# A new global order of all steps in a two-block transformer kernel, with 66 instead of 428 filler matmuls

## What is computed

```python
x = L0_attn_x                                   # (16, 256, 128)
x = _layernorm(x + attn(x))                     # block 1
x = _layernorm(x + ffn(x))                      # block 2, seen as tokens in groups of (s, h) = (128, 128)

def attn(x):                                    # 16 query heads, 4 key/value heads, 8 wide
    q, k = rope(rms_norm(x @ w_q)), rope(rms_norm(x @ w_k)); v = x @ w_v
    s = tanh(q @ k.T / sqrt(8) / 50) * 50       # causal
    return (softmax(s) @ v) @ w_o

def ffn(x):                                     # 16 heads, not causal, then 8 experts
    hn = layernorm(x) * ln1_g + ln1_b
    x = x + softmax(q @ k.T / sqrt(8)) @ v @ wo + bo     # q, k, v from hn
    hn2 = layernorm(x) * ln2_g + ln2_b
    idx = argmax(hn2 @ gate_w + gate_b)         # one expert of 8 for each token
    return x + (relu(hn2 @ w1[idx] + b1[idx]) @ w2[idx] + b2[idx])
```

## Time and profile before

| | before |
|---|---|
| median of 3 runs | 726.37 us (725.46 to 730.91) |
| span of the profiled execution | 701.0 us |
| busy: PE / DVE / ACT / POOL | 570.1 / 480.9 / 425.4 / 416.7 us |
| TensorE matmuls | 5771 |
| mean granted TensorE clock | 0.927 |

### The profile page before, as it was taken

How to read it: one execution, slowest core, us unless ns; L and a number is a source line. 1 busy time by engine, 2 the same in 40 slices (tenths; PEclk the granted TensorE clock), 3 DMA queues, 4 the chain that set the end, 5 groups by cost and what they waited for, 6 DMA issues and landing times.

```text
span 701.0 us, 16358 instructions
## 1 busy us (share of the span) xinstructions
PE 570.1 (81%) x5771; PEld 339.1 (48%) x5771; DVE 480.9 (69%) x1356; ACT 425.4 (61%) x650; POOL 416.7 (59%) x443
## 2 busy tenths in 40 slices
PE   2648888888888878888897898878997899888992
PEld 1324333344445444455454554545553555557992
DVE  3546757868678868587867768687777787635452
ACT  1675376676785666757677596756675654534661
POOL 2469573648486953775757585769544235525664
PEclk9969779899999988799999999899998999999996
DMA  6420000000000100000012301001002022186650
GB/s 146 135 69 2 8 1 9 2 24 1 9 2 25 40 2 6 5 16 10 17 41 62 85 9 36 1 20 60 25 29 62 12 69 91 39 257 183 187 149 6
DMA packets 30143, 34.30 MB, mean 49 GB/s; under 512 B 6970, under 2 KB 21984, under 8 KB 30064
## 3 DMA queue, kind: packets, MB, share of 16 engines
q1 hardware_dynamic: 26096, 25.53, 12.9%
q0 software_dynamic: 2816, 6.43, 2.6%
q10 hardware_dynamic: 1152, 1.30, 0.6%
HBM read 22.37 MB, written 11.27 MB: 48 GB/s over the span
## 4 chain that ended last, share of the span: by engine, by line
PE 40%; DVE 23%; POOL 16%; issue 10%; ACT 7%; SPq 2%; DMA 1%; POOLq 0%; ACTq 0%; DVEq 0%
DVE mx L1230 10%; PE out L877 6%; POOL rs L1411 5%; PE ring_s L863 3%; POOL stack L1414 3%; PE out L762 3%; PE ring_p L943 3%; PE ring_p L701 3%; PE ring_s L843 3%; POOL p L1430 2%; ACT p L1004 2%; PE ring_p L814 2%; ACT p L973 2%; PE ring_s L749 2%; PE ring_p L931 1%
## 5 line engine op out<-in xcount | busy, mean ns | idle before, releaser
L1230 DVE TENSOR_REDUCE mx<-ring_s 128x4 f32<-128x1024 f32 x128 | 152.8, 1218 | 26.9 <-PE ring_s L843 26.1
L1004 ACT ACTIVATE p<-ring_s 128x1024 f32<-128x1024 f32 x128 | 126.3, 1027 | 38.8 <-PE ring_s L863 38.3
L973 ACT ACTIVATE p<-ring_s 128x1024 f32<-128x1024 f32 x96 | 97.1, 1022 | 38.5 <-PE ring_s L749 38.1
L1411 POOL TENSOR_TENSOR rs<-ms,small 128x40 f32<-128x40 f32 x14 | 94.8, 6772 | 27.6 <-DVE ms L1093 27.3
L1414 POOL TENSOR_SCALAR stack<-stack 128x256 f16<-128x256 f16 (+1 forms) x96 | 65.0, 700 | 75.7 <-DVE stack L1222 42.8
L1430 POOL TENSOR_SCALAR_AFFINE_SELECT p<-p 128x512 f32<-128x512 f32 (+1 forms) x96 | 75.8, 798 | 56.4 <-ACT p L977 56.3
L977 ACT ACTIVATE p<-p 128x1024 f32<-128x1024 f32 x96 | 100.2, 1057 | 0.7
L701 PE MATMUL ring_p<-blank 128*128 128x256 f16 x362 | 80.6, 286 | 5.1 <-ACT t_midT L1037 1.9
L877 PE MATMUL out<-p,v 128*32 128x256 f32 x1024 | 69.8, 400 | 1.3 <-DVE rb L1288 1.2
L843 PE MATMUL ring_s<-kc,qs 32*128 32x256 f16 x512 | 51.2, 281 | 20.2 <-DVE mx L1230 13.0
L863 PE MATMUL ring_s<-qs,kc 32*128 32x256 f16 x512 | 49.4, 290 | 10.1 <-DMA qs<-mT 4.5
(11 more groups left out here) (162 smaller groups left out, 1111.5 us busy)
## 6 DMA issues: line engine op xcount, KB each, us to landing
w_up<-in_L_ffn_w SPq DMA_DIRECT2D x40, 256.0 KB, 2.8
t_row<-routed_rows SPq DMA_DIRECT2D x40, 132.0 KB, 2.4
routed_rows<-padrow SPq DMA_DIRECT2D x8, 396.0 KB, 3.2
xs<-in_L_attn_x SPq DMA_DIRECT2D x16, 128.0 KB, 2.2
routed_rows<-padrow SPq DMA_DIRECT2D x8, 132.0 KB, 1.9
qs<-mT SPq DMA_DIRECT2D x64, 2.0 KB
out<-t_y,t_idx POOLq DMA_INDIRECT x40, 2.4
b_down<-in_L_ffn_b SPq DMA_DIRECT2D x1, 512.0 KB, 4.8
```

What stands on the lines that cost most here:

```text
L973: nc.scalar.activation(p1[:, u], bank(f"b_sc{u}", n)[:], ACT.Tanh, scale=float(ISQ / CAP)).then_inc(b_s.sem, 1)
L1004: nc.scalar.activation(p2[:, u], bank(f"e_sc{u}", n)[:], ACT.Exp, scale=float(ISQ)).then_inc(e_s.sem, 1)
L1230: nc.vector.tensor_reduce(mx2[:, t, 2 * pair:2 * pair + 2, 2 * k:2 * k + 2], bank(f"d_mx{j}", n)[:].rearrange("p (z g s) -> p z g s", z=2, ...
L1411: nc.gpsimd.tensor_tensor(rs1[:], ms1[:], half, ALU.pow).then_inc(a_p.sem, 1)
```

## The change

`ORDER` is replaced by another one for the same steps. The list has 2481 entries in place of 2843: 66 `w_fill` in place of 428, and each other step once as before. With the fillers left out of both lists, a TensorE step stands 2.0 places from where it stood on the mean (21 at most), a DVE step 1.3, an ACT step 1.5, a POOL step 2.0 and an SP step 2.4. Neither the plans, the rings, the buffers nor any computation is changed.

In `g_row` the wait for scatters is now made for each slot and not only for a plan's first: for the two latest `f_scatter` that stand ahead of it in the order. `scattered` collects them.

The diff, cut to the lists that the prediction speaks of (the others are replaced in the same way):

```diff
--- before.py
+++ after.py
@@ -121,190 +121,171 @@
 ORDER = {
-    "w_fill": (10, 29, 30, 42, 49, 60, 67, 88, 99, 100, 112, 136, 152, 154, 159, 164, 169, 181, 185, 197, 202, 203,
-        206, 209, 214, 240, 241, 282, 284, 296, 297, 298, 301, 302, 303, 305, 309, 310, 314, 323, 325, 326, 331, 342,
...
-    "a_pow": (82, 168, 275, 396, 516, 658, 884, 978, 1167, 1283, 1519, 1639, 1822, 1957),
-    "f_place": (409, 532, 684, 835, 977, 1134, 1289, 1433, 1621, 1853, 2008, 2127, 2286, 2376, 2508, 2591),
-    "f_scatter": (477, 732, 878, 879, 1122, 1317, 1413, 1444, 1854, 2005, 2033, 2126, 2400, 2427, 2519, 2598),
-    "p_plan": (1442, 2134, 2512, 2605),
-    "g_w": (1472, 1482, 1567, 1574, 1590, 1611, 1699, 1744, 1765, 2139, 2159, 2175, 2332, 2340, 2341, 2352, 2387,
-        2505, 2515, 2570, 2578, 2589, 2600, 2607, 2608, 2648, 2651, 2676, 2681, 2690, 2697, 2715, 2722, 2737, 2757,
-        2780, 2784, 2801, 2814, 2821),
-    "g_row": (1473, 1481, 1486, 1560, 1572, 1599, 1643, 1726, 1759, 2106, 2166, 2171, 2200, 2331, 2342, 2359, 2366,
-        2526, 2528, 2545, 2572, 2583, 2595, 2612, 2618, 2634, 2641, 2642, 2660, 2680, 2692, 2699, 2701, 2714, 2738,
-        2742, 2768, 2772, 2789, 2822),
-    "g_up": (1521, 1523, 1661, 1828, 1902, 1951, 1973, 2076, 2132, 2260, 2315, 2336, 2383, 2426, 2451, 2465, 2504,
-        2563, 2564, 2603, 2614, 2617, 2637, 2644, 2667, 2677, 2683, 2687, 2706, 2718, 2726, 2743, 2755, 2764, 2774,
-        2792, 2795, 2806, 2817, 2824),
-    "g_down": (1608, 1632, 1771, 1842, 1972, 2068, 2079, 2105, 2168, 2289, 2373, 2415, 2421, 2463, 2510, 2533, 2548,
-        2590, 2604, 2615, 2624, 2639, 2646, 2668, 2678, 2685, 2696, 2719, 2724, 2728, 2750, 2756, 2769, 2783, 2793,
-        2802, 2812, 2819, 2828, 2837),
-    "q_sp": (2552,),
...
+    "w_fill": (14, 69, 88, 89, 90, 107, 112, 165, 216, 236, 246, 270, 271, 291, 329, 370, 423, 527, 528, 546, 561,
+        574, 580, 628, 645, 675, 718, 753, 862, 895, 913, 915, 1059, 1060, 1122, 1241, 1269, 1308, 1348, 1366, 1458,
+        1510, 1511, 1543, 1544, 1547, 1642, 1684, 1685, 1686, 1824, 1831, 1851, 1861, 1899, 1913, 1914, 2113, 2149,
+        2228, 2257, 2266, 2267, 2269, 2349, 2468),
+    "a_pow": (72, 148, 231, 392, 492, 615, 760, 867, 1007, 1146, 1272, 1410, 1569, 1653),
+    "f_place": (378, 490, 625, 755, 872, 1001, 1120, 1235, 1409, 1575, 1734, 1835, 1987, 2080, 2161, 2241),
+    "f_scatter": (516, 570, 671, 810, 974, 1006, 1144, 1252, 1495, 1762, 1828, 1839, 2005, 2097, 2168, 2252),
+    "p_plan": (1236, 1841, 2163, 2245),
+    "g_w": (1265, 1283, 1264, 1538, 1263, 1539, 1364, 1413, 1341, 1957, 2009, 1846, 1848, 2032, 1879, 1881, 2033,
+        2177, 2178, 2187, 2184, 2219, 2188, 2250, 2251, 2255, 2295, 2294, 2318, 2292, 2319, 2329, 2354, 2331, 2360,
+        2368, 2367, 2390, 2429, 2455),
+    "g_row": (1267, 1281, 1282, 1340, 1362, 1363, 1365, 1399, 1412, 1847, 1849, 1850, 1880, 1935, 1939, 1950, 1956,
+        2169, 2179, 2185, 2186, 2212, 2220, 2253, 2256, 2293, 2298, 2299, 2316, 2324, 2330, 2332, 2353, 2355, 2357,
+        2366, 2384, 2387, 2408, 2453),
+    "g_up": (1310, 1311, 1441, 1576, 1637, 1667, 1707, 1786, 1855, 1981, 2013, 2030, 2068, 2091, 2123, 2156, 2174,
+        2218, 2222, 2244, 2268, 2270, 2282, 2286, 2307, 2314, 2321, 2339, 2351, 2359, 2373, 2383, 2396, 2405, 2413,
+        2421, 2427, 2437, 2451, 2469),
+    "g_down": (1394, 1401, 1532, 1592, 1690, 1771, 1793, 1809, 1878, 2008, 2059, 2078, 2093, 2135, 2164, 2189, 2197,
+        2236, 2258, 2259, 2273, 2287, 2291, 2308, 2322, 2333, 2342, 2356, 2371, 2378, 2394, 2403, 2412, 2418, 2434,
+        2443, 2450, 2452, 2470, 2476),
+    "q_sp": (2217,),
...
@@ -588,6 +569,13 @@
             elif name in ON_TENSOR or name[:4] in ("b_sc", "d_mx", "e_sc"):
                 shape = "full"
 
+        scattered, so_far = {}, []
+        for name, n in order:
+            if name == "f_scatter":
+                so_far.append(n)
+            elif name == "g_row":
+                scattered[n] = tuple(so_far)
+
         def bank(name, n):
             k = ring_of(name, n)
             return ring[k][turn[name, n] % RINGS[k]]
@@ -642,10 +630,9 @@
             def g_row(s):
                 k = plan_of(s)
                 sp.wait_ge(r_v.sem, r_v.upto(k, "row"))
+                for n in scattered[s][-2:]:
+                    wait_turn(sp, rows_out[n % 2], n, 2, 16 * T)
                 if s == PLANS[k][1]:
-                    last = PLANS[k][0]
-                    for n in (last - 1, last):
-                        wait_turn(sp, rows_out[n % 2], n, 2, 16 * T)
                     if k >= LAST:
                         sp.wait_ge(pads_out, 16 * E)
                         sp.wait_ge(idle_rows, 16 * IDLE)
```

More of the change, by code:

```diff
@@ new lines @@
+    "g_rs": (1437, 1500, 1620, 1643, 1761, 1779, 1819, 1840, 2037, 2046, 2096, 2132, 2137, 2165, 2182, 2201, 2224,
+        2242, 2262, 2276, 2283, 2297, 2301, 2323, 2338, 2343, 2350, 2370, 2381, 2388, 2400, 2410, 2420, 2432, 2441,
+        2448, 2457, 2462, 2473, 2478),
+    "g_y": (1460, 1580, 1696, 1727, 1798, 1803, 1821, 1858, 2040, 2050, 2100, 2138, 2142, 2170, 2196, 2203, 2254,
+        2260, 2263, 2278, 2289, 2302, 2311, 2325, 2341, 2352, 2362, 2374, 2386, 2401, 2407, 2416, 2426, 2439, 2444,
+        2456, 2461, 2465, 2474, 2479),
@@ L308 @@
+    "g_out": (1509, 1619, 1763, 1733, 1877, 1895, 1894, 1876, 2056, 2058, 2167, 2183, 2166, 2237, 2248, 2213, 2275,
+        2285, 2265, 2284, 2296, 2317, 2344, 2337, 2363, 2369, 2380, 2382, 2389, 2402, 2430, 2433, 2431, 2442, 2449,
+        2460, 2464, 2466, 2475, 2480),
+    "q_sp": (2217,),
 }
```

146 lines of the change are left out of this document (67 added, 79 removed), and 154 rows, old and new, of the table ORDER.

## The result

| | kernel before | changed kernel |
|---|---|---|
| runs beside each other, us (median, lowest to highest) | 727.48 (725.46 to 730.91) | 674.85 (672.62 to 680.48) |
| ratio of the times | | 0.930 [0.925, 0.934] |
| profiled execution: span, mean granted clock | 701.0 us, 0.927 | 670.9 us, 0.869 |

A forecast was written before the change was run, and what follows sets the result against it. Engines waiting for each other in a fixed order, none full, were taken as the bound; -15 (fillers) + 8 (clock) - 2 (end) = -9 us gave a span of 692, plus 25.4 outside it: 717 us, range 702 to 738.

The forecast's parts named there:

- What bounds the kernel: Whole kernel: no engine full, engines waiting for each other in a fixed order; TensorE's real work some 473 us.
- The order of the steps: All queues: the two lists nearly one without fillers, no better or worse coupling shown; taken as 0.
- one `a_pow` more or less: GpSimd's power step on the path: bounds of the order term, 6.8 us either way.
- order couples worse: Rival, all queues: `a_pow`'s 6.8 us on the path in three places more, 738 us; chance 0.08.
- The fillers that go: TensorE's path: 362 fillers fewer, taken as 15 us gained, bounds 5 and 21.
- The clock: TensorE's clock: five more falls of 6.5 us at 0.25 us each us, 8 us lost; bounds none and twenty falls.
- the clock decides: Rival, TensorE's clock: 66 fillers don't hold it, so slower; 738 us with eighteen falls; chance 0.14.
- The rule of the Trainium skill: Rival, TensorE's clock: penalty half of the throttled time; five falls cost 16 us, forecast 725; chance 0.07 with few falls.
- The end: SP queue after plan 14: less backlog gives 3 us, late `f_scatter(15)` takes 1; -2, bounds -4 and +2.
- The waits: `g_row` on SP: 80 waits in place of 8 that will not wait; taken as 0, +1.7 kept for the range.
- The base: Whole run: median of the runs taken as 25.4 us above the profiled span, so 692 became 717 us.
- What the profile was to show: Profile after: fillers under 5 us on chain, PE busy near 500, clock 0.90 to 0.93; wrong if under 0.87.

The follow-up runs named there:

- b_nofill: Kernel before with all 428 fillers taken out of the old list, nothing else: 708.6 us, ratio 1.010.
- a_nofill: Changed kernel (new list) without its 66 fillers: 675.0 us, ratio 0.960 to the kernel before.
- a_fill428: New list with the old list's 428 fillers put in, 45 of them a little later: 697.3 us, ratio 0.994 to the kernel before.
- The mixtures: Lists without fillers, read by the kernel before, with some engines' or the experts' steps as in the new list, the others as in the old: 754.2 to 812.5 us.
- m_pool: Kernel before without fillers, GpSimd's steps in the new order, other engines in the old (some pairs turned): 754.2 us, ratio 1.029.
- m_pooldve: Kernel before without fillers, GpSimd's and VectorE's steps in the new order, other engines in the old (some pairs turned): 790.2 us, ratio 1.088.
- a_oldwait: Changed kernel with the old wait rule in `g_row` (only at a plan's first slot): 677.7 us, ratio 0.967 to the kernel before.
- b_nopow: Kernel before without fillers, `a_pow` multiplying instead of raising to a power: 722.0 us, ratio 0.999.
- a_nopow: New list without fillers, `a_pow` multiplying instead of raising to a power: 675.4 us, ratio 0.937 to the kernel before.
- r_pe: Kernel before without fillers, only TensorE's steps moved by a few places, found by a replay of the waits: 714.7 us, ratio 1.018.
- s_b12a: Without fillers, all engines in the old order up to `d_mT` of batch 12, then the new: 706.7 us, ratio 0.974 to the kernel before.

## Why the prediction was wrong

- **What bounds the kernel** was read rightly: no engine is full, and the time is how the engines wait for each other in a fixed order. The next steps did not follow from it: most of the working went into fillers and clock, and the order got one paragraph. The 473 us of real work for TensorE was too low: the fillers' records overlap the others', and without them it is 527.
- **The order of the steps, taken as 0 with bounds of 6.8 us, is the step that failed.** It is worth 33.6 us without fillers (`b_nofill` against `a_nofill`) and 6.6 with 428 in both lists (the kernel before against `a_fill428`). With it failed the adding up: the forecast gave fillers, clock and order a term each, and what fillers and clock are worth turned out to depend on the order (taking all 428 out costs the old list 4.7 us and gains the new one 22.3). Two measures were taken from the lists, the steps between two uses of a `ring_s` buffer (115 and 108 pairs close together) and the distance from `d_mT` to `e_sc0` (5.4 and 6.0). Both look inside one engine or one batch. What neither sees is between the queues: which steps of other batches and slots stand at the head while a step behind them is ready. The mixtures speak for this as the place of the change; step by step it was not shown. "Steps move by one to two and a half places on the mean" was taken as small; `m_pool` and `m_pooldve` differ from the old list by about that on one or two engines, beside the pairs that were turned, and took 6 and 11% more than its 709 us. The bound by "one `a_pow` more or less" had no ground, and the rival "order couples worse" stood alone: its mirror image, couples better, was not among the rivals though nothing excluded it.
- **The fillers that go, -15,** came to -19 by the chain: on it they went from 24.6 us to 5.7. Their cover was thinner than I took it to be, and the upper bound of 21 was nearer.
- **The clock, +8,** is mis-sized by its count, not by its price. The price of 0.25 us for each us at the lower clock came out at 0.28 to 0.30 in the estimates above. But the low time rose by 74 us (102 to 176), not by the 33 of five falls: it is some +22. "The real work moves closer together" was to hold the clock in the fillers' place and did so only in part. Together the two terms are +3 in place of -7 if the order is changed last; directly, `b_nofill` less what the 66 fillers bring says +3 to +6. The rival "the clock decides" had the mechanism, though not the sign, since the order outweighs it. The rule of the Trainium skill (TensorE: Matmul & The Clock Gate, section on HAM oscillation), a penalty of half of the throttled time, does not hold for this kernel: it would make 50 us of the 101 where the pair of runs gives 29 to 31.
- **The end, -2,** came to 0. The mechanism was as told (ten fetches, then the padding, then the scatter), but nothing ahead of it was gained: 67.3 us from the scatter to the end in both.
- **The waits, 0,** were right (`a_oldwait`); the trace has 39 of them on the SP queue in place of 3, of 17 ns each in the median.
- **The base.** The forecast put 25.4 us on top of the span as "outside" it. Only 1.7 us are; the rest was that the profiled execution and the timed runs of the kernel before belong to its two levels. Beside the upper one the change gained 52.6 us, beside the lower one 31. The experiments account for the 31; the other 21 are the upper level itself, which the changed kernel doesn't have, and they stay open. Set on the span alone, with 2 us around it, the forecast would have been 694 us, 19 above the 675 measured. The order's -34, the +10 of fillers and clock and the +2 of the end make -22 of that; the 3 that are left over are within the scatter of the runs.
- **What the profile was to show:** a sixth of the fillers' records, 5.7 us of them on the chain (under 5 were told) and the late scatter came about as told. The mean clock of 0.869 is just under the 0.87 given as a sign of a wrong clock term: that sign showed. TensorE's busy time is 549 and not near 500, for the overlap named above. The sign "an unchanged PE share with longer waits for DVE" did not show: its share rose from 40 to 46%, and the idle time ahead of DVE's row maxima fell from 26.9 to 23.3 us.

What is left open: which steps of batches 9 to 12 make the 22 us. One queue of GpSimd does not (`m_pool`), its long instruction does not (`b_nopow`, `a_nopow`), and `r_pe`, which was to test TensorE's queue, kept its idle time. Open too is why the kernel before has two levels, 704 and 722 to 727 us, by the chip; no trace of the upper one was taken. Without fillers the old list does not show it up to batch 12 (511.8 us in `s_b12a` on a chip of the upper level, 515.2 and 511.2 on chip A), so the fillers may have a part in it; that was not tested. None of the other kernels beat the changed one by more than the scatter.

## What to carry to other kernels

Where a kernel is a fixed order of steps over several queues and no engine is full, the order is the first term of the sum, not the last: a new list in which each step moves by only a couple of places was worth 5% without fillers, and a list in which two engines follow another order than the rest was 7 to 15% slower, by either way of reckoning. Nor can an order and the fillers that were placed for it be priced one by one: with the old fillers the same new list was worth 1%. Before a price of 0 is given to an order, give the case that it gets better the same room as the case that it gets worse. The idle time of a queue in which a later step was ready (here 20 us against 10 in one stretch) says where to look, not what will be gained. And set the span of a profiled execution against runs of the same chip before a difference is called "outside the span".

## What the runs showed of the hardware

- A us at the lower clock cost some 0.3 us here and not half of itself: 0.30 and 0.29 by the two pairs of lists with and without fillers, 0.28 between executions of the same kernel. All three are estimates from measured times and clocks. Holding the clock with filler matmuls brought a little more than it cost in the old list (24.6 us on the chain for 30) and much less in the new (40 for 18). The changed kernel, with which only kernels of its own list are level, has 176 us at the lower level.
- In the stretch from batch 8 to 12 the list that packs the work more closely had a clock of 0.89 to 0.93 without a filler, the other 0.80 to 0.88; over the whole span they had 0.855 and 0.857.
- Records of matmuls overlap: fillers busy for 97 us by themselves raise TensorE's busy time only from 527 to 570.
- GpSimd's 128x40 product takes 257 ns where the same instruction as a power takes 6773: 26 times as long.
- The same program, the kernel before, takes 704 us on two chips (mean clock mostly 0.92 to 0.94) and 722 to 725 on three others (0.90 to 0.92), while the changed one takes 673 to 675 beside either level.
